# Mixture of experts with its shares applied before the down projection, on a tuned three-part kernel

## The reference

```
xn    = layernorm(x)                                   # per token
score = sigmoid(xn @ router.T)                         # 16 per token
top8  = the 8 largest of score + bias
w[e]  = 2.826 * score[e] / sum(score of the 8)  if e in top8 else 0
y_e   = (silu(xn @ gate_e.T) * (xn @ up_e.T)) @ down_e.T
x     = x + y_shared + sum_e w[e] * y_e
```

## Time and profile before

| | us |
|---|---|
| median of 3 runs | 3724.94 (3723.39 to 3729.19) |
| profiled execution | 3718.72 |
| its span, first to last instruction | 3717.0 |
| PE busy in the span | 3420.2 (92%) |
| DVE busy | 2662.9 (72%) |
| ACT busy | 1684.2 (45%) |
| POOL busy | 901.7 (24%) |

### The profile page before, as it was taken

The page is one execution under the profiler, slowest core; times in us unless marked ns, Lnnn a source line. Parts: engine busy times, 40 slices in busy tenths (PEclk is TensorE's granted clock), DMA queues, the critical chain, the costliest instruction groups (busy, mean ns, idle before and its releaser), DMA issues. The chain is left out here.

```text
span 3717.0 us, 106102 instructions
## 1 busy us (share of the span) xinstructions
PE 3420.2 (92%) x43480; PEld 2611.4 (70%) x43480; DVE 2662.9 (72%) x6886; ACT 1684.2 (45%) x3438; POOL 901.7 (24%) x781
## 2 busy tenths in 40 slices
PE   4999999999999999799949999999999999977998
PEld 2777777777777777688836777767677777756887
DVE  3666666666666666688867888888788887857887
ACT  1555555555555555433324444444444444423332
POOL 3323332223323322100002223322332233320000
PEclk9999999999999999899979999999999999988999
DMA  2000000000000000000000000000000000000000
GB/s 89 28 27 28 25 28 28 24 30 26 28 27 28 24 24 24 7 1 0 0 15 17 3 17 3 3 17 3 17 3 3 17 3 3 3 2 1 1 1 23
DMA packets 38391, 60.20 MB, mean 16 GB/s; under 512 B 6960, under 2 KB 16688, under 8 KB 37552
## 3 DMA queue, kind: packets, MB, share of 16 engines
q1 hardware_dynamic: 37936, 53.78, 4.2%
HBM read 18.10 MB, written 2.10 MB: 5 GB/s over the span
## 5 line engine op out<-in xcount | busy, mean ns | idle before, releaser
L663 ACT ACTIVATE a_prob<-a_s,a_shift,a_scale 128x128 f32<-128x128 f32 (+3 forms) x512 | 312.2, 614 | 526.2 <-DVE a_shift L746 526.2
L1548 ACT ACTIVATE ffn_silu<-ffn_ps_g 128x512 f32<-128x512 f32 x272 | 161.3, 599 | 383.7 <-PE ffn_ps_g L1498 371.1
L1491 PEld LDWEIGHTS ffn_ps_y<-moe_down,ffn_hidden 128*128 128x128 f32 x2176 | 282.1, 191 | 41.5 <-issue 20.0
L1491 PE MATMUL ffn_ps_y<-moe_down,ffn_hidden 128*128 128x128 f32 x2176 | 288.1, 275 | 17.4 <-DVE ffn_acc L1652 17.4
L946 POOL TENSOR_TENSOR t_rstd<-t_var_eps,minus_half 128x4 f32<-128x4 f32 x96 | 97.6, 1017 | 792.0 <-DVE t_var_eps L1261 792.0
L1199 ACT COPY t_num<-t_n 128x512 f32<-128x512 f32 x96 | 56.3, 586 | 491.9 <-PE t_n L1007 491.4
L1652 DVE SCALAR_TENSOR_TENSOR ffn_acc<-ffn_ps_y,ffn_combine,ffn_acc 128x128 f32<-128x128 f32 x960 | 269.8, 345 | 7.5
L1664 DVE TENSOR_TENSOR ffn_hidden<-ffn_silu,ffn_ps_u 128x512 f32<-128x512 f32 x272 | 185.5, 684 | 108.7 <-ACT ffn_silu L1548 74.5
L1337 DVE TENSOR_TENSOR t_mixed<-t_s,upto 128x512 f32<-128x512 f32 x384 | 238.4, 684 | 15.7 <-PE t_s L983 13.8
L408 POOL TENSOR_TENSOR a_k_sin<-a_k_swap,sin_swap 128x512 f32<-128x512 f32 x64 | 81.4, 1272 | 669.9 <-DMA a_k_swap<-a_k_own 669.9
L983 PE MATMUL t_s<-t_phi_q,t_kz 32*128 32x64 f32 x6144 | 210.0, 277 | 31.1 <-DVE t_hid L1368 16.5
(11 more groups left out here) (210 smaller groups left out, 8501.1 us busy)
## 6 DMA issues: line engine op xcount, KB each, us to landing
a_k_swap<-a_k_own SPq DMA_DIRECT2D x128, 128.0 KB, 2.1
a_y_swap<-a_y_own SPq DMA_DIRECT2D x128, 128.0 KB, 2.0
a_staged<-in_pairs SPq DMA_DIRECT2D x8, 384.0 KB, 3.1
t_next<-in_t_w SPq DMA_DIRECT2D x12, 256.0 KB, 3.2
t_next_rows<-in_t_rows SPq DMA_DIRECT2D x6, 448.0 KB, 4.1
x<-in_x SPq DMA_DIRECT2D x8, 256.0 KB, 5.1
out<-x SPq DMA_DIRECT2D x1, 2048.0 KB, 8.7
t_next_sq<-in_t_sq SPq DMA_DIRECT2D x6, 256.0 KB, 2.7
```

The lines of the kernel that those rows point to most:

```text
L663: nc.scalar.activation(prob[c % 2][h][:, 0:(c + 1) * P], ps[f"s{h}"][:, 0:(c + 1) * P], ACT.Exp, bias=shift[:, k:k + 1], scale=scale[slot. ...
L1491: t = nc.tensor.matmul(ps_y[e % 2][:, c * P:(c + 1) * P], hidden[e % 3][:, c * P:(c + 1) * P], w_down[:, e * P:(e + 1) * P], start=True, s ...
```

## The change

Expert stage:

- The loop over groups is written out; one set of semaphores serves both expert stages. The shared expert comes first in a group.
- The shares of the tokens are transposed (`turn_shares`, 4 transposes), copied (`copy_shares`), written to DRAM (`spread`) and read back by SP, one DMA an expert, as a row of 512 shares repeated on all 128 partitions, into a ring of 6 buffers `shares`.
- GpSimd multiplies silu by the shares (`weighed`); the shared expert skips this.
- VectorE writes weighed x up back into the bank of the up projection, of which there are three. ScalarE rounds it to `h_hi`, VectorE subtracts to `h_lo`, and the down projection is three f32r matmuls of 512 columns that accumulate over all 17 experts in one bank `ps_y` of the group, three experts behind. The down weights are split too.
- At the end of a group: one copy to `yT`, four transposes `back`, one add.
- The statistics of the first group come ahead of the splitting of the weights, which goes expert by expert (shared, 0 to 3, 4 to 7, 8 to 15). `route` is done in 16 matmuls on strips of 32 tokens.
- Preparing steps have places by expert (`due`): in the steady part stats 15, aggregate 16, power 0, xn 1, turn 5, copies 6, x_lo 7, route 9, scores 16, choose 0 to 4 of the next group, turn_shares 7, copy_shares 8.

Transformer stage: kz is made by ScalarE, as Exp of banks s2 and s3 with a bias of 0 or -1e30 by partition, in a step of its own behind h1. F1 fills s0, s1, n1 and w1; VectorE takes the relu of f = 0, 1 and 3, ScalarE that of f = 2.

```diff
-    FILLS = dict(... F1="s0 s1 s2 s3", F2="w1")
+    ACT = "turn att project mapq A1 mapk h1 kz weights F1 A0".split()
+    FILLS = dict(... F1="s0 s1 n1 w1", F2="w1")
...
                     elif step == "S0":
-                        wait(pe, "kz", slot, 2)
+                        ready("s2", "mapk")
                         for bank in ("s0", "s1"):
                             ready(bank, "mapq")
...
+                    elif step == "kz":
+                        for t_, bank in enumerate(("s2", "s3")):
+                            for p in range(2):
+                                t = nc.scalar.activation(kz[t_][:, :, p, :],
+                                                         ps[bank][:].rearrange("p (u n) -> p u n", u=SPANS), ACT.Exp,
+                                                         bias=mem["strip_bias"][:, p:p + 1])
+                            t.then_inc(emptied[bank], 1)
...
-                        for f in (1, 3):
+                        for f in (0, 1, 3):
...
-                    elif step == "mapk":
-                        for t_ in range(2):
-                            wait_emptied(dve, f"s{2 + t_}", slot, "mapk")
-                            for p in range(2):
-                                nc.vector.tensor_scalar(kz[t_][:, :, p, :],
-                                                        phi_k[t_][:].rearrange("p (u n) -> p u n", u=SPANS),
-                                                        mem["strip_head"][:, p:p + 1], None,
-                                                        ALU.mult).then_inc(s["kz"], 1)
```

```diff
+            @block.sync
+            def _(sp):
+                for g in range(first, last):
+                    sp.wait_ge(comb_done, g + 1)
+                    sp.dma_start(spread[g % 2], combT[:]).then_inc(spread_done, 16)
+                    sp.wait_ge(spread_done, 16 * (g + 1))
+                    for e in range(E):
+                        k = g * E + e
+                        if k >= first * E + RING:
+                            sp.wait_ge(weighed_done, k - RING + 1)
+                        sp.dma_start(shares[k % RING][:], spread[g % 2, e:e + 1, :].squeeze(0).partition_broadcast(P)
+                                     ).then_inc(share_done[k % RING], 16)
...
+                def down(n):
+                    g, i = divmod(n, N)
+                    at = slice(expert(i) * P, (expert(i) + 1) * P)
...
+                    pe.wait_ge(lo_done, n + 1)
+                    if i == 0 and g >= 2:
+                        pe.wait_ge(group_done, g - 1)
+                    pe.nop(nofuse=True)
+                    for k, (w, h) in enumerate(((down_hi, h_hi), (down_hi, h_lo), (down_lo, h_hi))):
+                        t = nc.tensor.matmul(ps_y[g % 2][:], w[:, at], h[n % 3][:], start=i == 0 and k == 0,
+                                             stop=i == N - 1 and k == 2, skip_group_check=True)
+                    t.then_inc(down_done, 1)
...
+                for n in range(start, end + BEHIND):
...
+                        if n >= 2:
+                            pe.wait_ge(silu_done, n - 1)
+                        up(ps_g[n % 2], gate_hi, gate_lo, n).then_inc(g_done, 1)
+                        if n >= 3:
+                            pe.wait_ge(lo_done, n - 2)
+                        up(ps_u[n % 3], up_hi, up_lo, n).then_inc(u_done, 1)
+                    if n == start + 1:
+                        turn_shares(first)
+                    if n >= start + BEHIND:
+                        down(n - BEHIND)
...
+                for n in range(start, end + 1):
...
+                        nc.scalar.activation(silu[n % 2][:], ps_g[n % 2][:], ACT.Silu).then_inc(silu_done, 1)
...
+                    if n > start:
+                        high(n - 1)
+                    if g == first and i in (2, 3):
+                        for k in range(3 * i, 3 * i + 3):
+                            split(k)
...
+                    if i:
+                        k = weighed_by(n) - 1
+                        pool.wait_ge(silu_done, n + 1)
+                        pool.wait_ge(share_done[k % RING], 16 * (k // RING + 1))
+                        if n >= 2:
+                            pool.wait_ge(hid_done, n - 1)
+                        pool.nop(nofuse=True)
+                        nc.gpsimd.tensor_tensor(weighed[n % 2][:], silu[n % 2][:], shares[k % RING][:],
+                                                ALU.mult).then_inc(weighed_done, 1)
...
+                def low(n):
+                    dve.wait_ge(hi_done, n + 1)
+                    if n >= 3:
+                        dve.wait_ge(down_done, n - 2)
+                    dve.nop(nofuse=True)
+                    nc.vector.tensor_tensor(h_lo[n % 3][:], ps_u[n % 3][:], h_hi[n % 3][:].bitcast(F32),
+                                            ALU.subtract).then_inc(lo_done, 1)
...
+                    nc.vector.tensor_tensor(ps_u[n % 3][:], (weighed if i else silu)[n % 2][:], ps_u[n % 3][:],
+                                            ALU.mult).then_inc(hid_done, 1)
+                    if n > start:
+                        low(n - 1)
```

More of the change, by code:

```diff
@@ L1409, in bank @@
             return ctx.enter_context(nc.psum_tensor(tag + name, [P, 512], F32))
-        def sem(name):
-            return ctx.enter_context(nc.semaphore(tag + name))
+        N = E + 1
+        last = first + groups
+        start, end = first * N, last * N
+        BEHIND = 3
+        RING = 6
         stats = sb("stats", [P, TILES, 6])
@@ L1684, in build @@
+                low(end - 1)
+                add(last - 1)
 def build(nc, ins, out, stages):
```

411 lines of the change are left out of this document (248 added, 163 removed).

## The result

| kernel | median, us | lowest to highest | runs |
|---|---|---|---|
| before | 3724.16 | 3720.04 to 3729.19 | 4 |
| the change | 3676.98 | 3671.95 to 3681.56 | 4 |

The ratio is 0.9873, with a 95% interval of 0.9856 to 0.9891: 47 us faster. The predicted time was 3672, so the forecast of case (a) holds to 5 us.

What follows compares the result with a forecast made beforehand. TensorE was taken to bound the kernel. Two expert stages at 19.5 us (17.7 + 0.3 + 1.5) give 39, keys 14, together 53 off the profiled 3718.72: 3665.7, plus 6.2 for the median, 3672 us; range 3640 to 3707.

Steps and rivals of the forecast that it cites:

- case (a): Whole kernel: TensorE stays the bound and stalls as summed, 3672 us; chance 0.50.
- Part 1: Steady expert: nine f32r matmuls at 0.2295 us give a period of 2.065 us instead of 2.27.
- The slack of about 0.4: Steady expert's loop over four engines: about 4.2 us needed, 4.82 less 0.2 available before the up projection.
- Part 2: Interruptions per steady group: 2.2 us stall, 1.77 other TensorE work; group 39.1 instead of 42.03, 17.7 us gained a stage.
- The reading of the port pair: Expert stage: VectorE operations with one PSUM input never wait for GpSimd; those with two SBUF inputs contend.
- Part 3: Start of an expert stage, up to the second group: 57.0 us against 57.3, gain 0.3, bounds -5 and +5.
- Part 4: End of an expert stage: last group 42.4 us against 43.9, gain 1.5.
- Part 5: Transformer keys: S0 loses its wait for VectorE's hid, 0.3 us in 48 slots, 14 us, bounds 0 and 20.
- (b): Expert stages: slack covers the interruptions, stall 0.6 us a group instead of 2.2, 3648 us; chance 0.20.
- (c): Expert stages: four-engine chain costs 0.3 to 0.5 us more, stall 4.5 a group, 3707 us; chance 0.19.
- (d): Expert stages: share broadcasts arrive too slowly, at 2.6 us a share the kernel takes 3767 us; chance 0.06.
- (e): Expert stages gain nothing, only the keys do: 3711 us, or 3725 with these lost too; chance 0.05.

Runs made afterwards that it cites:

- experiment 11: Changed kernel with only xn of the third group moved from place 12's predecessor, place 9, to place 12: median 3671.36 us, ratio 0.9868.
- experiment 3: Kernel before with only the feed-forward's banks changed to s0 s1 n1 w1, keys still padded by VectorE: median 3725.55 us, ratio 1.0008.
- experts-only kernel: Kernel before with only the new expert stages, transformer old: median 3696.11 us, ratio 0.9925.
- experiment 6: Changed kernel with GpSimd's product reading constant tiles, the share broadcasts and their waits left out: 3678.68 us in one run.
- keys-only kernel: Kernel before with only the new transformer (keys padded by ScalarE, new feed-forward banks), expert stages old: median 3704.20 us, ratio 0.9952.

## Why the prediction was right, point by point

- **Part 1, the steady expert.** 2.065 was 2.08: the spacing is 0.231, not 0.2295. 0.27 us a group too little. The slack of about 0.4 holds: the loop measures 4.52 with late weights, the up projection comes 2 x 2.08 + 0.69 = 4.85 behind.
- **Part 2, interruptions.** 2.2 us a group were 1.37. The sigmoid's 0.8 measured 0.67. The rest of the list (0.75 for xn and max, 0.35 for the choice, 0.3 for x_lo) has 0.7 of 1.4: chosen and x_lo are held (x_lo takes 1.74 us), but within the slack. TensorE's extras, 1.77, were 1.87. Group: 39.1 predicted, 38.62 measured. The reading of the port pair was right on both sides: hid and low stay at or below 0.697 us in 217 records between 1609 and 1850, select and x_lo are held.
- **Part 3, the start: the step that failed.** Up to expert 6 it holds: first gate projection 7.4 (7.2), third up projection 21.6 (21.8), expert 6 at 30.9 (30.3). Behind it the text went on with "Then 11 experts, the other groups' routing and one stall": 26.7 us. They took 61.95 - 30.9 = 31.05, with about 6.7 us of late up projections and slow matmuls where the text allowed 2.2. The splits were priced at 0.6 for 512 columns, the time of a kernel in which GpSimd was idle beside them. Two input tiles in SBUF make them what Part 2 had said is held, and the rule was applied to the steady group only. The 6.7 are the late up projection behind the splits (2.2, with a recorded wait of 1.88), a granted clock of 0.66 in the 5 us behind 1560, after that wait (1.6: eight matmuls 0.43 apart instead of 0.23), a later wait (1.0, recorded 0.60), and the collision of xn and the choice (2.0; 2.4 by experiment 11). The bounds of Part 3, -5 and +5, just hold it.
- **Part 4, the end.** 42.4 for the last group, measured 42.4, by some luck: its list adds up to 8.15, not 8.3. The gain of 1.5 was 0.7, since the group of before was 43.1, not 43.9.
- **Part 5, the keys.** 14 us, and the medians say 12 to 23. The number is in range and its mechanism half: 0.17 a slot, 8 us, is the wait for S0, behind which lay 0.18 of TensorE's own, and experiment 3 takes this wait away without any gain in the median. The other part are pauses that the text did not know of, in the transformer and, with the old expert stage, at VectorE's loop.
- **Rivals.** (b) had the stalls too low (0.6 for 1.37), (c) too high (4.5). (d) is out: shares land 3.3 us after issue, but six are under way at once, and leaving them out changes no steady group. (e) is out by the experts-only kernel. The chances for a faster kernel add up to 0.91 to 0.92, where the text has 0.90.
- **The sum.** Experts 34.2 of 39 by the stages of the two profiles, keys 12 to 19 of 14: the parts sum to 46 to 53, the medians say 47. That the forecast is only 5 us off is partly luck: in the first stage the steady groups gave 4.0 more than predicted (21.7 for 17.7) and the start 5.0 less (-4.65 for 0.3).

## What to carry to other kernels

Before work is moved to GpSimd, list every VectorE operation with two SBUF inputs that will run beside it, the ones at a stage's start too, and price each with up to one GpSimd operation on top; here that was 2.3 us for 1.2, and 1.2 for 0.2. The list needs the tensor_scalar with one SBUF input as well: a piece of xn took 0.77 instead of 0.34 in the changed kernel, 1.30 in experiment 6. Remove a hole only after looking at what comes next: without its wait for the shares the start of the stage got 1.5 us shorter, as xn, held by the products, and then the splits stood behind it, while putting splits into the hole and choosing earlier gained 6 us in the two stages and moving one xn another 6. Read the groups of a loop one by one before taking their mean: 42.03 hid a pause of VectorE in every second group. A stage whose length differs by 19 us between kernels with the same code there (1458.2 to 1477.0) needs medians of several runs, and an edit there is priced by those, not by a pair of profiles.

## What the runs showed of the hardware that I had not expected

- The hold works both ways. GpSimd's two products took 2.49 us beside VectorE operations with a PSUM input and 3.58 beside VectorE's splits.
- A matmul that resumes behind a wait costs more than the wait: a recorded 0.31 us was 0.47 to the start of the up projection, and the next matmul came 0.34 behind it instead of 0.23.
- An fp32 matmul of 512 columns behind f32r ones cost about 0.85 us of TensorE's period (2.24 less six spacings of 0.23), where three f32r ones cost 0.69. The Trainium skill (FP8 and Floating Point Precision, TensorE Precision Notes) speaks of four passes for true fp32, by which an estimate would be 4 x 0.23 = 0.92; the trace is a little below.
- Every fourth S0 of the kernel before pauses in the middle of 64 equal matmuls. Its cause stays open.
- VectorE stood idle for 2.35 to 2.65 us at the start of a loop iteration, with nothing recorded that it waited for, in both expert stages of before; in the same loop of the keys-only kernel it did so in the first stage and not in the second (0.02 us). Its cause stays open too.
